# Batch attention with routing: constant part of the rows in six transfers, x statistics behind the subtraction, last groups one by one, semaphores cleared elsewhere

## The chip, the cores and the metric

The kernel runs on one core of one Trainium2 chip. The metric is the device time in microseconds (us) of one execution. The core has five engines that matter here: PE (TensorE, matrix products; its weight loads are PEld), DVE (VectorE), ACT (ScalarE), POOL (GpSimd) and SP (SyncE), which here only starts transfers. Transfers are started from the queues of SP, ACT and POOL and done by 16 DMA engines.

## The reference, cut to what matters

Two transformer layers with adaptive layer norm. The part that the change touches is the last half layer: attention over the batch axis (for each position, 16 rows attend to each other in 4 heads), layer norm, and a router that sends every one of the 8192 tokens to one of 8 experts.

```python
def _mha(x, Wqkv, bqkv, Wo, bo):            # x is (S, B, D), D = 128, hd = 32
    q, k, v = split(x @ Wqkv.T + bqkv)      # attention over B for each head
    att = softmax(einsum('bhqd,bhkd->bhqk', q, k) / sqrt(hd))
    return einsum('bhqk,bhkd->bhqd', att, v) @ Wo.T + bo
...
logits = xf @ Wg.T
idx = jnp.argmax(logits, axis=-1)
for e in range(E):                          # E = 8
    m = (idx == e)[:, None]
    h = relu(xf @ W1[e] + b1[e]);  out = out + m * (h @ W2[e] + b2[e])
```

## The kernel before, in words

`build` (line 2024) puts the stages one after the other: `prologue`, `attention` of layer 0, `token_shift_ffn`, `attention` of layer 1, `clear_semaphores`, `attend_and_route`, `run_experts`. Each stage is a block of its own: every engine has its own written program, all engines meet at the block's end, and the next block starts from there. `clear_semaphores` (line 2058) is a block with one instruction on POOL, which resets the semaphores that earlier stages have given back.

`attend_and_route` (line 1126), here called the stage, takes the 8192 tokens as 16 groups (0 to 15) of 4 tiles of 128 x 128. It is a software pipeline written out by hand: `run` (in the stage) counts steps s from -4 to 20, and each engine has a step function that serves several groups at once. In step s, ACT normalises group s+4 (`act_xn`), POOL scales and shifts it (`pool_scale`, `pool_h`) and prepares the residual of group s+3 (`pool_xb`), PE computes the scores of group s (`pe_scores`), q, k and v of group s+2 (`pe_qk`, `pe_v`), then the values and the output product of group s-1 (`pe_values`, `pe_out`). DVE starts the step with the rows of group s-2 (`vec_u`, line 1403), their statistics, then the softmax of group s: maximum, subtraction, (ACT takes the exponential, `act_exp`), sum, reciprocal, product, 32 x 32 transpose. The transposed probabilities go through four transfers on SP's queue (`sp_ax`, line 1366, tile ax), and `pe_values` waits for them. The bias-corrected k goes through four transfers of `sp_kx` (line 1295). Every engine does its instructions strictly in the order written, so one waiting instruction holds up all behind it.

The routing goes over rounds r of two groups each: `act_rstd` (step 2r+3), `vec_choose` (a chain of eight small DVE operations that ends in a running count, line 1450; step 2r+4), `pe_rank` (two products, step 2r+4), `vec_dest` (the row numbers, line 1472; step 2r+5). From step 5 on POOL sends the finished rows of group s-5 with `pool_row` (line 1492), four scatters of 128 rows for each group. A row has 387 numbers: u, three small ones, the residual, and a constant part gw. From step 12 (`s >= G - 4`) POOL does the scatters with waits on PE's progress between them (lines 1566 to 1577).

Two more jobs lie in the pipeline. The constant part gw is spread over all 24 slots of the ring S by a single transfer on ACT's queue at the end of ACT's step 0 (line 1537, 1.5 MB); steps 1 to 7 then send one block of padding rows each. And the layer norm statistics of x, needed by `act_xn`, are computed on DVE ahead of steps (`x_stats` in the vector program): a `bn_stats` for each tile by the table `x_groups`, and at four points (`PARTS`) six small operations (`vec_x_stats`) with two ACT activations in the middle (`act_stats`), for which ACT then waits.

Of the kernel before, what the change touches and what calls it, by code (L numbers as in the profile page):

```python
# [25 lines left out]
ALU = mybir.AluOpType  # L26
# [4 lines left out]
P = 128  # L31
TPB = T // P
NT = B * TPB
# [257 lines left out]
def attention(nc, A, K, layer):  # L291
# [8 lines left out]
    sh, scl = (SA0, CA0) if layer == 0 else (SA1, CA1)  # L300
    with ExitStack() as ctx:
# [421 lines left out]
        with nc.Block() as block:  # L723
# [83 lines left out]
            def _(pool):  # L807
                if layer == 1:
                    pool.tensor_tensor(K.gw[:, :], K.rows[:, 2, :], K.tab[:, 2, :], ALU.mult).then_inc(gw_ready, 1)
                    for t in range(3):  # L810
                        pool_rope(pool, 0, t)
# [314 lines left out]
def attend_and_route(nc, A, K, slot_row, expert):  # L1126
# [6 lines left out]
    G = NT // 4  # L1133
    UG, RG, VG = 7, 6, 5
    with ExitStack() as ctx:
# [11 lines left out]
        half = lambda r: slice(8 * (r % 2), 8 * (r % 2) + 8)  # L1147
# [41 lines left out]
        ones_set, gate_in, pads_out, pads_ready = sem("ones_set"), sem("gate_in"), sem("pads_out"), sem("pads_ready")  # L1189
# [4 lines left out]
        by_e = lambda t: t.unsqueeze(2).to_broadcast([P, 8, E])  # L1194
        ring = lambda g: slice(4 * (g % RG), 4 * (g % RG) + 4)
        pair = lambda r: slice(8 * (r % (RG // 2)), 8 * (r % (RG // 2)) + 8)
        held = lambda g: slice(4 * (g % UG), 4 * (g % UG) + 4)

        PARTS = [(-3, 2, 4), (-2, 4, 6), (1, 6, 10), (4, 10, 16)]
        x_groups = {-3: [2, 3], -2: [4, 5], -1: [6, 7], 0: [8], 1: [9], 2: [10, 11], 3: [12, 13], 4: [14, 15]}  # L1200

        def act_stats(act, part, n):
# [5 lines left out]
            act.wait_ge(rstd_ready, part + 1)  # L1208

        def vec_x_stats(v, part, n):  # L1210
# [8 lines left out]
            v.tensor_tensor(K.diff[:, n], mean0, mean1, ALU.add).then_inc(var_ready, 1)  # L1219
            v.wait_ge(std_ready, part + 1)  # L1220
# [4 lines left out]
        def act_xn(act, g):  # L1225
            wait(act, h1_ready, g)
            for t in range(4):
# [200 lines left out]
        def act_rstd(act, r):  # L1428
            act.wait_ge(var_done, 8 * r + 8)
            act.activation(uln[:, :], umv[:, half(r), 1], ACT.Ln, bias=K.eps[:, 0:1]).then_inc(uln_ready, 1)  # L1430
            act.wait_ge(uln_ready, r + 1)
            act.activation(S[:, pair(r), RS], uln[:, :], ACT.Exp, scale=-0.5).then_inc(rstd_done, 1)

        def vec_choose(v, link, r):

            ties = tie[:, :].unsqueeze(1).to_broadcast([P, 8, E])
            v.wait_ge(lg_ready, 2 * r + 2)
            v.wait_ge(rstd_done, r + 1)
            wait(v, pos_ps, r)
            v.wait_ge(sm_ready, min(2 * r + 5, G))  # L1440
            v.scalar_tensor_tensor(out=S[:, pair(r), MR], in0=umv[:, half(r), 0], scalar=-1.0, in1=S[:, pair(r), RS],
                                   op0=ALU.mult, op1=ALU.mult).then_inc(mr_done, 1)
            link(v.tensor_tensor(lg, raw[:, half(r), :], by_e(S[:, pair(r), RS]), ALU.mult))
            link(v.tensor_tensor(lg, lg, c8[:, :].unsqueeze(1).to_broadcast([P, 8, E]), ALU.add))
            link(v.tensor_reduce(best[:, :], lg, AX.X, ALU.max))
            link(v.tensor_tensor(lg, lg, by_e(best[:, :]), ALU.is_ge))
            link(v.tensor_tensor(lg, lg, ties, ALU.mult))
            link(v.tensor_reduce(first, lg, AX.X, ALU.max))
            link(v.tensor_tensor(hot[:, :, 1:9].rearrange("p e n -> p n e"), ties, by_e(first), ALU.is_equal))
# [3 lines left out]
        def pe_rank(pe, r):  # L1453

            pe.wait_ge(hot_ready, r + 1)
            if r == 0:
                pe.wait_ge(tab_in, 5 * 16)
                pe.wait_ge(ones_set, 1)
# [634 lines left out]
```

## Time and profile before

| What | us |
|---|---|
| median of 3 runs (1055.21 to 1058.4) | 1056.24 |
| the profiled execution | 1061.03 |
| its span, first to last instruction | 1059.2 |
| `attend_and_route`, first instruction to last scatter issue | 684.9 to 881.1 |
| `run_experts`, first transfer to the end | 889.5 to 1059.2 |

The rows of the views give the start of an instruction or of a merged group in us from the start of the span, its busy time, the engine, the source line, the operation and its tiles. In brackets stands how long the engine was idle before it and what ended that idle time. PE's granted clock stands as a share of full speed (1.0 is 2.4 GHz, 0.5 is 1.2 GHz). "issue" means that nothing in the profile shows what the engine waited for.

### The profile page before, as it was taken

To read this page: it belongs to the slowest core of one execution; us is meant where nothing else is said; L and a number is where in the kernel's file an instruction comes from. 1 tells how busy PE (TensorE), PEld (TensorE's weight loads), DVE (VectorE), ACT (ScalarE), POOL (GpSimd) and SP (SyncE) were. 2 spreads that over 40 slices of the span, in tenths; PEclk is the share of its full clock that TensorE was granted. 3 is DMA by queue.
4 is the path that set the end of the run, shared out by engine and by line. 5 is a ranking of instruction groups with operands and counts; after the bars stand their busy time and mean duration, and the time that the engine had idled before them with its cause. 6 is when DMAs were issued, how large, how long until landed. Compare 5 with 4: busy or idle time off the path is not lost. (4 is left out here: it accounts for less than half of the span.)

```text
span 1059.2 us, 25374 instructions
## 1 busy us (share of the span) xinstructions
PE 864.7 (82%) x5236; PEld 617.7 (58%) x5236; DVE 865.7 (82%) x2839; ACT 630.7 (60%) x1634; POOL 722.7 (68%) x626
## 2 busy tenths in 40 slices
PE   5699999999968858888889898377888631999993
PEld 4466666666546635555555555245565421999993
DVE  5599999999967967888889898657899760899995
ACT  2655555555349945767676766375665202999992
POOL 4488888888832228999999999373588462255554
PEclk9899999999989979999999999678899755999997
DMA  8520000000000000000000000273466554544420
GB/s 242 174 55 1 0 0 0 0 0 0 1 4 1 1 0 2 20 10 20 10 20 10 20 10 20 87 192 101 128 193 189 171 194 131 161 129 132 131 71 20
DMA packets 64855, 70.11 MB, mean 66 GB/s; under 512 B 8885, under 2 KB 52098, under 8 KB 64660
## 3 DMA queue, kind: packets, MB, share of 16 engines
q1 hardware_dynamic: 50612, 47.20, 16.1%
q0 software_dynamic: 6368, 16.89, 4.6%
q10 hardware_dynamic: 7792, 5.08, 1.9%
q8 instruction: 32, 0.52, 0.2%
q14 instruction: 51, 0.42, 0.1%
HBM read 32.32 MB, written 24.50 MB: 54 GB/s over the span
## 5 line engine op out<-in xcount | busy, mean ns | idle before, releaser
L472 PE MATMUL a_pS<-a_kv,utri 128*128 128x360 f32 (+3 forms) x768 | 264.8, 481 | 17.9 <-POOL a_kv L463 10.0
L463 POOL TENSOR_TENSOR a_kv<-a_qk,a_vv 128x1152 f32<-128x1152 f32 (+1 forms) x128 | 264.1, 2064 | 13.3 <-DVE a_qk L437 13.3
L472 PEld LDWEIGHTS a_pS<-a_kv,utri 128*128 128x128 f32 x768 | 136.1, 190 | 99.6 <-issue 25.3
L568 POOL TENSOR_TENSOR a_tt<-a_tt 128x576 f32<-128x576 f32 (+1 forms) x128 | 156.9, 1226 | 49.5 <-DVE a_tt L552 45.7
L552 DVE TENSOR_TENSOR a_tt<-a_pS,a_qk 128x360 f32<-128x360 f32 (+3 forms) x384 | 180.8, 526 | 10.8 <-PE a_pS L472 7.8
L1896 POOL DMA_INDIRECT out_dram<-x_o,x_place x71 | 69.1, 973 | 77.1 <-DVE x_o L1883 76.2
L580 DVE TENSOR_REDUCE a_nd<-a_tt 128x144 f32<-128x720 f32 (+3 forms) x128 | 104.3, 815 | 0.0
L518 ACT ACTIVATE a_tt<-a_pI 128x144 f32<-128x144 f32 (+1 forms) x96 | 40.1, 417 | 105.4 <-PE a_pI L480 105.3
L1492 POOL DMA_INDIRECT ys<-m_S,m_dest x64 | 63.6, 993 | 39.6 <-DVE m_dest L1472 15.1
L511 PEld LDWEIGHTS a_pO<-wgate,a_yT 128*128 128x128 f32 x256 | 44.8, 193 | 75.3 <-issue 45.3
L511 PE MATMUL a_pO<-wgate,a_yT 128*128 (+1 forms) x256 | 54.8, 296 | 31.0 <-POOL a_yT L542 22.7
L1834 PE MATMUL x_pZ<-w,x_hT 128*128 x568 | 76.5, 278 | 1.4 <-issue 1.3
L1785 ACT ACTIVATE x_w<-w 128x644 f32 x71 | 52.4, 741 | 34.0 <-PEq L1604 28.6
L1834 PEld LDWEIGHTS x_pZ<-w,x_hT 128*128 128x128 f32 x568 | 69.7, 193 | 2.1 <-issue 2.1
L409 ACT ACTIVATE a_vv<-a_pQ 128x128 f32<-128x128 f32 x122 | 33.8, 277 | 55.2 <-PE a_pQ L400 53.3
L371 ACT ACTIVATE a_xn<-X,nmr,rstd 128x128 f32 (+1 forms) x128 | 60.9, 485 | 2.0 <-DVE nmr L275 1.8
L287 DVE BATCH_NORM_STATS2 bn<-X 128x6 f32<-128x128 f32 (+1 forms) x256 | 57.4, 277 | 1.2 <-DMA X<-xs 1.1
L400 PE MATMUL a_pQ<-W,a_hT 128*128 128x384 f32 x122 | 51.5, 504 | 4.2 <-ACT a_hT L387 2.5
L455 POOL TENSOR_TENSOR a_qk<-a_ra,a_rb 128x256 f32<-128x256 f32 x64 | 46.8, 731 | 9.3 <-DVE a_rb L448 9.3
L400 PE MATMUL a_pQ<-wqkv,a_hT 128*128 128x384 f32 x122 | 50.3, 494 | 1.5 <-ACT a_hT L387 1.5
L480 PEld LDWEIGHTS a_pI<-a_R,a_qT 128*128 128x128 f32 x192 | 34.4, 189 | 28.3 <-ACT a_qT L524 11.2
L1816 ACT ACTIVATE x_hT<-x_pA,x_w 128x128 f32<-128x128 f32 x142 | 44.0, 362 | 9.1 <-PE x_pB L1808 9.1
(297 smaller groups left out, 2192.6 us busy)
## 6 DMA issues: line engine op xcount, KB each, us to landing
x_yl<-ys SPq DMA_DIRECT2D x71, 193.5 KB, 2.4
X<-xs SPq DMA_DIRECT2D x16, 256.0 KB, 5.2
kx<-m_kc SPq DMA_DIRECT2D x64, 64.0 KB
ax<-m_pc SPq DMA_DIRECT2D x64, 64.0 KB
m_S<-X SPq DMA_DIRECT2D x16, 256.0 KB, 2.8
xs<-X SPq DMA_DIRECT2D x15, 256.0 KB, 2.3
w<-in_L_ffn_W_dram SPq DMA_DIRECT2D x1, 2048.0 KB
m_S<-gw ACTq DMA_DIRECT2D x1, 1536.0 KB, 11.0
```

Of the source, the lines that this page charges most:

```text
L287: v.bn_stats(K.bn[:, ds(n, 1), :].rearrange("p a f -> p (a f)"), x[:, ds(n, 1), :].rearrange("p a f -> p (a f)"))\
L371: act.activation(xn[:, t, :], tile(K.X, 4 * b + t), ACT.Identity, bias=column(K.nmr, 4 * b + t), scale=column(K.rstd, 4 * b + t)).then_inc ...
L400: pe.matmul(bank_of(b, t, start)[:, 0:3 * P], hT[:, t * P:(t + 1) * P], wqkv, start=True, stop=True).then_inc(qkv_ps, 1)
L463: pool.tensor_tensor(kv[:, t % 2, :, :, :], kk.unsqueeze(2).to_broadcast([P, H, J, D]), vv[:, t, :, :].unsqueeze(3).to_broadcast([P, H, J, ...
L472: pe.matmul(pS[c][:, 0:(h1 - h0) * SC], K.utri[:, :], flat[:, h0 * SC:h1 * SC], start=True, stop=True).then_inc(u_done, 1)
L511: pe.matmul(pO[:, 0:P], yT[:, :], tile(K.wgate[:, 0 if layer == 0 else 2, :, :], b), start=True, stop=True).then_inc(proj_ps, 1)
L552: v.tensor_tensor(tt[:, t % 2, h0:h1, :, 0:D], pS[c][:, 0:(h1 - h0) * SC].rearrange("p (h j i) -> p h j i", i=D, j=J), q[:, h0:h1, :].unsq ...
L568: pool.tensor_tensor(tt[:, t % 2, :, :, D // 2:D], tt[:, t % 2, :, :, D // 2:D], tt[:, t % 2, :, :, 0:D // 2], ALU.add).then_inc(half_done, 1)
L580: v.tensor_reduce(nd[:, t % 2, :, :], tt[:, t % 2, :, :, D // 2:rows], AX.X, ALU.add).then_inc(red_done, 1)
L1492: pool.indirect_dma_start(out=A["ys"], out_offset=bass.IndirectOffsetOnAxis(ap=dest[:, g // 2 % 2, at:at + 1], axis=0), in_=S[:, 4 * (g % ...
L1834: mm = pe.matmul(pZ[j % 2][:, 0:P], hT[:, j % 2, c * P:(c + 1) * P], K.w2[:, ds(e, 1), c, :].rearrange("p a f -> p (a f)"), start=(c == 0) ...
L1896: pool.indirect_dma_start(out=token_rows, out_offset=bass.IndirectOffsetOnAxis(ap=place[:, j:j + 1], axis=0), in_=o[:, j % 4, :], in_offse ...
```

## The change

Four edits, all around `attend_and_route`:

1. The constant part gw is written in six transfers of 4 ring slots (256 KB), one at the end of ACT's steps 0 to 5, each with a semaphore of its own; the seven padding transfers move from steps 1 to 7 to steps 6 to 12.
2. The x statistics move. `bn_stats` of x and the small operations before ACT's part now stand within DVE's step, behind the subtraction (and behind `vec_var`); the last of the six (`vec_x_offset`) stands at the end of the step. The parts come at steps -4, -3, -1 and 3 in place of ahead of -3, -2, 1 and 4. ACT computes its two activations at the end of its step and no longer waits there; `act_xn` waits for the part that it needs. The tables that were set ahead of step 3 are set ahead of step 0.
3. Groups 14 and 15 are rounds of their own (round 7 and round 8), each with half as wide operations. Round 6 (groups 12 and 13) is chosen at the end of DVE's step 15 in place of step 16. POOL's wait on `w_ps` is for 15 groups at most, not 16.
4. The block of `clear_semaphores` goes. POOL clears one set at the start of `attention` of layer 1 and the rest in the stage, behind its last scatter.

```diff
-            if s == 0:
-                act.dma_start(S[:, :, GO:], K.gw[:, :].unsqueeze(1).to_broadcast([P, 4 * RG, P])).then_inc(gate_in, 16)
-            if 0 < s <= SLOTS - NT:
-                at = E * CAP + P * (s - 1)
+            if 0 <= s < RG:
+                act.dma_start(S[:, ring(s), GO:], K.gw[:, :].unsqueeze(1).to_broadcast([P, 4, P])).then_inc(gate_in[s], 16)
+            if 0 <= s - RG < SLOTS - NT:
+                at = E * CAP + P * (s - RG)
                 act.dma_start(A["ys"][at:at + P, :], A["k_pad"]).then_inc(pads_out, 16)
...
-        PARTS = [(-3, 2, 4), (-2, 4, 6), (1, 6, 10), (4, 10, 16)]
-        x_groups = {-3: [2, 3], -2: [4, 5], -1: [6, 7], 0: [8], 1: [9], 2: [10, 11], 3: [12, 13], 4: [14, 15]}
+        PARTS = {-4: (0, 2, 4), -3: (1, 4, 6), -1: (2, 6, 10), 3: (3, 10, 16)}
+        x_groups = {-4: [2, 3], -3: [4, 5], -2: [6, 7], -1: [8, 9], 1: [10, 11], 2: [12, 13], 3: [14, 15]}
...
             act.activation(K.rstd[:, n], K.std[:, n], ACT.Exp, scale=-0.5).then_inc(std_ready, 1)
-            act.wait_ge(rstd_ready, part + 1)
...
         def act_xn(act, g):
             wait(act, h1_ready, g)
+            wait(act, rstd_ready, sum(1 for _, lo, hi in PARTS.values() if g >= lo))
...
         def vec_step(v, s, link):
...
-            if even(s - 5):
+            if even(s - 5) and s < G:
                 vec_dest(v, link, (s - 5) // 2)
...
             if there(s - 2):
                 vec_var(v, s - 2)
-            if even(s - 4):
+            x_stats(v, s)
+            if s in PARTS:
+                v.wait_ge(stats, 4 * (PARTS[s][2] - 2))
+                vec_x_var(v, *part_of(s))
+            if even(s - 4) and s < G:
                 vec_choose(v, link, (s - 4) // 2)
             if there(s):
                 vec_total(v, s)
                 vec_reciprocal(v, s)
                 vec_probs(v, s)
                 vec_transpose(v, s)
+            if s in PARTS:
+                vec_x_offset(v, *part_of(s))
+            if s == G or s == G + 1:
+                vec_dest(v, link, s - 10)
+            if G - 1 <= s <= G + 1:
+                vec_choose(v, link, s - 9)
+            if s == G + 1:
+                vec_dest(v, link, s - 9)
...
-                    pool.wait_ge(w_ps, min(s, G))
+                    pool.wait_ge(w_ps, min(s, G - 1))
                     pool_row(pool, s - 5, 3)
...
                 run(pool, pool_step)
+                clear_semaphores(pool, left)
                 for i in range(RG):
                     pool.wait_ge(rows_out[i], 64 * ((G - 1 - i) // RG + 1))
...
-        clear_semaphores(nc)
```

DVE's program before, from the end of step 2 to the first operation of step 4 (bn<-X are the statistics of x, m_S<-m_rows_ps,m_U is `vec_u`), with the softmax and statistics of step 3 left out between the two pieces:

```order
L1358 STREAM_TRANSPOSE m_pc<-m_pn 128x512
L287 BN_STATS bn<-X 128x6 x8
L1679 MEMSET m_reset 128x72
L1680 MEMSET m_reset 128x8
L1681 COPY m_hot<-m_caps 128x8
L1403 TENSOR_TENSOR m_S<-m_rows_ps,m_U 128x4x128
...
L287 BN_STATS bn<-X 128x6 x8
L1212 TENSOR_TENSOR diff<-bn 128x24
L1213 TENSOR_TENSOR var<-bn 128x24
L1215 SCALAR_TENSOR_TENSOR std<-diff 128x24
L1218 TENSOR_TENSOR var<-var,std 128x24
L1219 TENSOR_TENSOR diff<-bn 128x24
L1222 SCALAR_TENSOR_TENSOR nmr<-diff,rstd 128x24
```

DVE's program of the change, from the subtraction of step 3 (m_sm) to the first operation of step 4:

```order
L1339 TENSOR_TENSOR m_sm<-m_pS,m_mx 128x512
L1437 BN_AGGR m_umv<-m_ubn 128x2 x4
L287 BN_STATS bn<-X 128x6 x8
L1220 TENSOR_TENSOR diff<-bn 128x24
L1223 SCALAR_TENSOR_TENSOR std<-diff 128x24
...
L1350 TENSOR_REDUCE m_sum<-m_ex 128x16
L1357 RECIPROCAL m_pS<-m_sum 128x16
L1362 TENSOR_TENSOR m_pn<-m_ex,m_pS 128x512
L1369 STREAM_TRANSPOSE m_pc<-m_pn 128x512
L1232 SCALAR_TENSOR_TENSOR nmr<-diff,rstd 128x24
L1414 TENSOR_TENSOR m_S<-m_rows_ps,m_U 128x4x128
```

Nothing stands between the transpose of one step and `vec_u` of the next any more but one small operation in step 3; the statistics stand between the subtraction and the sum.

ACT's program before, at the end of step 0 and the start of step 1 (w is the scaling of an expert's weights, std and rstd are `act_stats`):

```order
L1259 ACTIVATE m_hT<-m_pT 128x512
L1497 ACTIVATE w<-w,cols 128x512
L1537 DMA m_S<-gw 128x24x128
L1205 ACTIVATE std<-var,eps 128x16
L1207 ACTIVATE rstd<-std 128x16
L1228 ACTIVATE m_xn<-X,nmr,rstd 128x128 x4
```

The same place in the change:

```order
L1270 ACTIVATE m_hT<-m_pT 128x512
L1517 ACTIVATE w<-w,cols 128x512
L1565 DMA m_S<-gw 128x4x128
L1239 ACTIVATE m_xn<-X,nmr,rstd 128x128 x4
```

The transfer has a sixth of its size, and the two activations have moved to the end of step -1.

DVE's program of the change in the last steps, with the chain of `vec_choose` shortened to its last operation (m_upto) and `vec_dest` to its cast (m_dest). The first m_upto is round 6, at the end of step 15; before, it stood behind m_umv of step 16:

```order
L1369 STREAM_TRANSPOSE m_pc<-m_pn 128x512
...
L1468 SCALAR_TENSOR_TENSOR m_upto<-m_reset,m_hot 128x72
L1414 TENSOR_TENSOR m_S<-m_rows_ps,m_U 128x4x128
...
L1437 BN_AGGR m_umv<-m_ubn 128x2 x4
...
L1492 CAST m_dest<-m_posf 128x8
```

The row numbers of groups 12 and 13 (m_dest) now come in step 16, one step earlier, and two rounds of one group each follow.

## Rows read from the trace of the kernel before

**Rows 1.** Busy time by stretch: PE, PEld, DVE, ACT, POOL, then clock, DMA share, GB/s
```profile
752.00:756.00 4.00, 4.00 (x36) 2.37 (x36) 3.86 (x16) 0.00 (x0) 0.58 (x1) 0.50 0.22 53
756.00:820.00 64.00, 55.14 (x682) 38.15 (x680) 57.18 (x172) 40.99 (x82) 56.36 (x51) 0.99 0.62 188
```

**Rows 2.** Timeline at two block starts: start, busy, engine, line, operation, idle before
```profile
381.94 0.48 DVE L777 MEMSET a_vv<- 128x512 f32 x1 [0.47 <-PEq L1077]
...
684.94 0.43 DVE L1676 TENSOR_TENSOR m_gb<-rows,tab 128x128 f32<-128x128 f32 x1 [1.56 <-PEq L2062]
```

**Rows 3.** DMA issues of the page: KB each, median us to landing
```profile
m_S<-X SPq DMA_DIRECT2D x16, 256.0 KB, 2.8
...
m_S<-gw ACTq DMA_DIRECT2D x1, 1536.0 KB, 11.0
```

**Rows 4.** Timeline of steps 0 and 1: ACT's queue, SP's queue, PE
```profile
706.75 0.75 ACTq L1537 DMA_DIRECT2D m_S<-gw  x1
709.10 5.86 SPq L1366 DMA_DIRECT2D ax<-m_pc  x4
...
713.10 1.21 PE L1275 MATMUL m_rows_ps<-wv,m_hT 128*128 128x136 f32 x8
718.17 1.93 PE L1377 MATMUL m_pO<-ax,m_v 128*32 128x128 f32 x32 [3.85 <-DMA ax<-m_pc]
```

**Rows 5.** Timeline of DVE and PE, from step 2 to the start of step 4
```profile
727.82 0.69 DVE L1339 TENSOR_REDUCE m_sum<-m_ex 128x16 f32<-128x512 f32 x1 [0.92 <-ACT m_ex L1334]
729.29 1.19 PE L1394 MATMUL m_rows_ps<-wo,m_oT 128*128 128x136 f32 x8 [0.22 <-ACT m_oT L1385]
730.20 1.60 DVE L287 BATCH_NORM_STATS2 bn<-X 128x6 f32<-128x128 f32 x8
...
733.28 0.69 DVE L1403 TENSOR_TENSOR m_S<-m_rows_ps,m_U 128x512 f32<-128x512 f32 x1
...
737.83 0.69 DVE L1339 TENSOR_REDUCE m_sum<-m_ex 128x16 f32<-128x512 f32 x1 [0.41 <-ACT m_ex L1334]
740.20 1.60 DVE L287 BATCH_NORM_STATS2 bn<-X 128x6 f32<-128x128 f32 x8
743.22 0.18 DVE L1222 SCALAR_TENSOR_TENSOR nmr<-diff,rstd 128x24 f32<-128x24 f32 x1 [0.52 <-ACT rstd L1207]
743.32 0.69 DVE L1403 TENSOR_TENSOR m_S<-m_rows_ps,m_U 128x512 f32<-128x512 f32 x1
```

**Rows 6.** Timeline of DVE: the same small operation with POOL busy and idle
```profile
691.09 1.21 DVE L1215 SCALAR_TENSOR_TENSOR std<-diff 128x8 f32<-128x8 f32 x1
...
742.18 0.18 DVE L1215 SCALAR_TENSOR_TENSOR std<-diff 128x24 f32<-128x24 f32 x1
```

**Rows 7.** Timeline of POOL: first scatter, and two steps' first product
```profile
755.42 1.19 POOL L1492 DMA_INDIRECT ys<-m_S,m_dest  x1 [6.33 <-DVE m_dest L1472]
756.64 1.28 POOL L1235 TENSOR_TENSOR m_U<-m_xn,tab 128x512 f32<-128x512 f32 x1
...
765.35 1.28 POOL L1235 TENSOR_TENSOR m_U<-m_xn,tab 128x512 f32<-128x512 f32 x1
```

**Rows 8.** Timeline of DVE and POOL in the last steps, and SP's start of the experts
```profile
850.63 0.69 DVE L1403 TENSOR_TENSOR m_S<-m_rows_ps,m_U 128x512 f32<-128x512 f32 x1 [1.99 <-PE m_rows_ps L1394]
852.56 0.14 DVE L1441 SCALAR_TENSOR_TENSOR m_S<-m_umv,m_S 128x8 f32<-128x8 f32 x1
854.50 0.31 DVE L1450 TENSOR_TENSOR_SCAN m_upto<-m_reset,m_hot 128x72 f32<-128x72 f32 x1
...
858.25 0.97 POOL L1492 DMA_INDIRECT ys<-m_S,m_dest  x1 [1.99 <-DVE m_S L1403]
860.57 0.97 POOL L1492 DMA_INDIRECT ys<-m_S,m_dest  x1 [1.35 <-DVE m_dest L1472]
880.14 0.98 POOL L1492 DMA_INDIRECT ys<-m_S,m_dest  x1 [0.30 <-issue]
...
889.54 21.68 SPq L1760 DMA_DIRECT2D x_yl<-ys  x20
```

More of the change, by code:

```diff
@@ L1133, in attend_and_route @@
     G = NT // 4
+    left = sorted(set(nc.released_uncleared_semaphores) - set(K.cleared))
     UG, RG, VG = 7, 6, 5
@@ L1146, in attend_and_route @@
         rc, lg, first = pS[:, 0:16], pS[:, 64:64 + 8 * E].rearrange("p (n e) -> p n e", e=E), pS[:, 128:136]
-        half = lambda r: slice(8 * (r % 2), 8 * (r % 2) + 8)
+        unit = lambda g: g // 2 if g < G - 2 else g - G // 2 + 1
+        groups = lambda r: [2 * r, 2 * r + 1] if r < G // 2 - 1 else [r + G // 2 - 1]
+        tiles = lambda r: 4 * len(groups(r))
+        span = lambda r, n: slice(4 * (groups(r)[0] % n), 4 * (groups(r)[0] % n) + tiles(r))
         xn = sb("xn", [P, 4, P])
@@ L1188, in attend_and_route @@
                                                             sem("mr_done"), sem("sum_ps"))
[L1189 removed]
+        ones_set, pads_out, pads_ready = sem("ones_set"), sem("pads_out"), sem("pads_ready")
+        gate_in = [sem(f"gate_in{i}") for i in range(RG)]
         xb_in, rows_out = [sem(f"xb_in{i}") for i in range(RG)], [sem(f"rows_out{i}") for i in range(RG)]
@@ L1219, in vec_x_stats, with vec_x_offset @@
             v.tensor_tensor(K.diff[:, n], mean0, mean1, ALU.add).then_inc(var_ready, 1)
+        def vec_x_offset(v, part, n):
             v.wait_ge(std_ready, part + 1)
@@ L1428, in act_rstd @@
         def act_rstd(act, r):
-            act.wait_ge(var_done, 8 * r + 8)
-            act.activation(uln[:, :], umv[:, half(r), 1], ACT.Ln, bias=K.eps[:, 0:1]).then_inc(uln_ready, 1)
+            n = tiles(r)
+            act.wait_ge(var_done, 4 * groups(r)[-1] + 4)
+            wait(act, rstd_done, r)
+            act.activation(uln[:, 0:n], umv[:, half(r), 1], ACT.Ln, bias=K.eps[:, 0:1]).then_inc(uln_ready, 1)
             act.wait_ge(uln_ready, r + 1)
-            act.activation(S[:, pair(r), RS], uln[:, :], ACT.Exp, scale=-0.5).then_inc(rstd_done, 1)
+            act.activation(S[:, pair(r), RS], uln[:, 0:n], ACT.Exp, scale=-0.5).then_inc(rstd_done, 1)
         def vec_choose(v, link, r):
-            ties = tie[:, :].unsqueeze(1).to_broadcast([P, 8, E])
-            v.wait_ge(lg_ready, 2 * r + 2)
+            n = tiles(r)
+            ties = tie[:, :].unsqueeze(1).to_broadcast([P, n, E])
+            lgn, mine = lg[:, 0:n, :], hot[:, :, 1:1 + n].rearrange("p e n -> p n e")
+            v.wait_ge(lg_ready, groups(r)[-1] + 1)
             v.wait_ge(rstd_done, r + 1)
@@ L1455, in pe_rank @@
             pe.wait_ge(hot_ready, r + 1)
+            wait(pe, pos_read, r)
             if r == 0:
@@ L1645, in _ @@
                 act.preload_act_table_set("natural_log_exp_and_others")
-                run(act, act_step, before={k: lambda part=part, lo=lo, hi=hi: act_stats(act, part, slice(4 * lo, 4 * hi))
-                    for part, (k, lo, hi) in enumerate(PARTS)})
+                run(act, act_step)
                 act.wait_ge(pads_ready, 3)
@@ L1691, in _ @@
                 run(v, lambda v, s: vec_step(v, s, link),
-                    before={**{k: lambda k=k: before_step(k) for k in range(-4, 6)}, 12: lambda: after_step(12)})
+                    before={0: set_tables, 12: lambda: after_step(12)})
                 v.wait_ge(sum_ps, 1)
@@ L2055, in build, with clear_semaphores @@
         run_experts(nc, A, K, slot_row, expert, out)
-def clear_semaphores(nc):
-    released = sorted(nc.released_uncleared_semaphores)
-    with nc.Block() as block:
-        @block.gpsimd
-        def _(pool):
-            start = 0
-            for i in range(1, len(released) + 1):
-                if i == len(released) or released[i] != released[i - 1] + 1:
-                    pool.sem_clear(range(released[start], released[i - 1] + 1))
-                    start = i
+def clear_semaphores(pool, released):
+    start = 0
+    for i in range(1, len(released) + 1):
+        if i == len(released) or released[i] != released[i - 1] + 1:
+            pool.sem_clear(range(released[start], released[i - 1] + 1))
+            start = i
 def kernel(**inputs):
```

96 lines of the change are left out of this document (52 added, 44 removed).

## The prediction, made before the changed kernel ran

> **What bounds the kernel now.** I read the busy time by stretch first, then the timeline of every engine inside the stage. In steps 5 to 11 POOL is the bound: it is busy 56.36 of 64 us [rows 1], with gaps of a few tenths between its instructions, and the same product comes again after 765.35 - 756.64 = 8.71 us, one step [rows 7]. DVE is close behind (57.18 of 64 us). Before that, POOL waits: its first scatter comes after 6.33 us of idling, until DVE has the first row numbers [rows 7]. So steps -4 to 4 are set by the chain that leads to the row numbers of round 0 (ACT, PE at a reduced clock, DVE), and an earlier first scatter moves the whole POOL-bound stretch with it. At the end, POOL again issues the last 16 scatters one every 1.28 us from 860.57 to 880.14 (19.57 / 15 = 1.30, one of them longer), and the experts' first transfer starts at 889.54 [rows 8]. So the questions are how much earlier the first scatter comes, and how much earlier the last run of 16 starts.
>
> I count the shift of each point against before; negative is earlier. "so far" is the running sum.
>
> **The block that goes.** DVE idles 0.47 us into the block of layer 1's attention, but 1.56 us into the stage, with the clearing block between [rows 2]. The difference, 1.1 us, is taken: so far -1.1. Bounds: 0 and -1.6. The clear itself now costs POOL one instruction at two places. In layer 1's attention it stands ahead of gw, which is not read before the stage; in the stage it stands behind the last scatter issue, where 889.54 - 881.12 = 8.4 us pass while rows land and the blocks change [rows 8]. Taken as 0; without that cover it costs at most the 1.1 us of the whole block, twice.
>
> **Steps -3 to 0.** `act_xn` of group 2 loses its wait for the statistics, which frees ACT, but PE's products set the next steps; I estimate 0.3 us gained. The two activations of part 2 now stand at the end of ACT's step -1, in a stretch where ACT has no slack: about 0.6 us lost (two activations and the wait between; half a microsecond is also what DVE waits for such a pair, 0.52 [rows 5]). The tables set ahead of step 0 fall in DVE's wait for the first scores. So far -0.8; bounds -2.0 (no loss, 0.9 gained) and -0.2.
>
> **Step 1, the 1.5 MB transfer.** It is issued at 706.75 and lands after 11.0 us, at about 717.8 [rows 3, 4]. The four ax transfers of step 0 are issued from 709.10, take 5.86 us to be issued, and PE's `pe_values` starts at 718.17, after 3.85 us of waiting for them [rows 4]: both land together. A piece of 256 KB should take about 2.8 us, as the residual of that size does [rows 3], so it is down before or just as the first ax starts. Late next is PE itself: it ends the v products at 713.10 + 1.21 = 714.3 [rows 4], and `pe_values` follows at once. That is 3.6 us earlier in addition to the 0.8: so far -4.4. Below, nothing (0) if something else holds ax; above, another 1.5 us if PE's clock rises sooner in the denser stretch.
> The Trainium skill speaks against this step: "DMA: Bandwidth & Descriptors", section on queues, rings and completion order, says that each DMA engine takes turns packet by packet between the queues that have work. By that rule ax, on another queue, would not wait for the end of gw. The trace does not look like it (both land at 718), but if ax is slow for a reason of its own, the 3.6 us stay; that is a rival below.
>
> **Step 2.** The statistics of two groups (1.60 us for 8 tiles [rows 5]) now stand between subtraction and sum, where DVE waited 0.92 us for the exponential [rows 5]. 1.6 - 0.9 = 0.7 lost.
> **Start of step 3.** PE has the product for `vec_u` at 729.29 + 1.19 = 730.48, but `vec_u` runs at 733.28, behind the statistics at 730.20 and the tables [rows 5]. These 2.8 us go. Late next is DVE's own transpose. So far -4.4 + 0.7 - 2.8 = -6.5.
> **Start of step 4.** From 740.20 to 743.32 stand statistics and part 3, 3.1 us, ahead of `vec_u` [rows 5]: gone. In their place step 3 gets 1.6 us of statistics and about 1.0 us of small operations (3.1 without the 0.52 us wait), against 0.41 us of waiting that they cover [rows 5]: 2.2 us added. Net -0.9. The five small operations read two tiles each, and with POOL busy such an operation took 1.21 us where it takes 0.18 with POOL idle [rows 6]. Before, part 3 ran while POOL was idle; now POOL works beside it. I take half a stall, 0.5 us; bounds 0 and 5 times 1.0 us. So far -6.5 - 0.9 + 0.5 = -6.9.
> The Trainium skill gives the stall as a rule ("SBUF — State Buffer", "SBUF: two separate sides"): VectorE and GpSimd share a port pair as an exclusive lock held for a whole instruction. The 1.21 against 0.18 us agree [rows 6]. By that rule an operation can wait for a whole POOL product.
>
> **Steps 4 to 15.** Step 4 and `vec_dest` of round 0 are unchanged, so the first scatter moves from 755.42 to about 748.5. From there POOL's 8.71 us a step hold, and the shift is carried. The padding transfers, now in steps 6 to 12, are as many as before and hide behind POOL; the 256 KB pieces of steps 1 to 5 take the place that they had. Taken as 0; at most 1 us, for an ax that comes later.
>
> **The tail.** The last scatter of group 11 waited for the product of group 15: 1.99 us idle where 0.30 is the plain gap [rows 8]. With 15 in place of 16 that wait is over: 1.7 us. The next scatter, the first of group 12, waited 1.35 us for the row numbers [rows 8]: 1.05 us more. Together 2.7 us, if the row numbers of round 6 are there by 860.57 - 2.7 = 857.9 (on the old clock). They are: the choice takes 852.56 to 854.81, 2.25 us [rows 8]. Put ahead of `vec_u` at 850.63 it fills the 1.99 us of idle time [rows 8] and delays `vec_u` by some 0.3 us; rank and `vec_dest` follow in step 16, at about 854. Rounds 7 and 8 add one more chain of 2.25 us and one `vec_dest`, with the scatters of group 14 due 8 x 1.28 = 10.2 us and of group 15 15.4 us after the start of the run, both late enough to hide them (round 8 is ready near 866, due at 873). So far -6.9 - 2.7 = -9.6. Bounds for the tail: 0, and -3.5.
>
> **The experts** are unchanged and start as much earlier.
>
> Sum: -1.1 + 0.3 - 3.6 + 0.7 - 2.8 - 0.9 + 0.5 - 2.7 = -9.6 us. Against its own time the profiled execution would go from 1061.03 to 1051.4; it lay 4.8 us above the median of the runs, so I take the same 9.6 us off 1056.24: 1046.6 us.
>
> **The rivals.**
> *A, the statistics collide with POOL.* Three or four of the small operations in steps -1 and 3 each wait for a whole POOL product [rows 6]: some 3.5 us given back. For it: DVE has no slack in step 3. Against: POOL is itself idle for half of each step here. 1050.1. By the skill's lock rule this is the case to expect when POOL is busy.
> *B, ax is not held by gw.* The engines take turns between the queues, the wait at 718.17 stays, and 3.6 us are not gained. For it: two different queues, and the issue itself is slow. Against: the two land together. 1050.2.
> *C, the tail gives nothing,* since landing of the rows or the extra round sets the end: 1046.6 + 2.7 = 1049.3. Against: nothing but 0.30 us gaps between the last scatters [rows 8].
> *D, slower.* In steps 5 to 11 PE is busy 55.14 of 64 us at clock 0.99 [rows 1], 7.5 us of a step of 8.71. Just before, the clock is 0.50, and 4 of 4 us are busy [rows 1]. If with the new timing the reduced clock reaches into these steps, PE needs some 15 us in such a step and becomes the bound, 6.3 us lost for each. From two steps on (12.6 us) the gain is gone; three give 1046.6 + 18.9 = 1065.5. For it: the clock falls to that level and rises again several times in this stage. Against: PE waits less than before.
> *E, no change:* early gains are absorbed by a wait that is not visible, such as x arriving, and the tail's too: 1056. Against: DVE and POOL themselves are the things waited for.
>
> **How the numbers follow.** Forecast 0.60 (its own range 1044.0 to 1049.0), A 0.15, B 0.10, C 0.07, D 0.05, E 0.03. The range that should hold the time 8 times in 10 takes in A, B and C and the larger gains of the bounds, not D and E: 1043.0 to 1051.0. A measurement of this kernel tells a change from none from about 0.3% on, 3.2 us. Forecast, A, B and C are all faster by more: 0.92. Same 0.03, slower 0.05.
>
> **What would show it.** Right: `pe_values` of step 1 with no long wait for ax, and near 713.8 in the new trace; `vec_u` of steps 3 and 4 straight behind the transpose; the first scatter near 748.5; 8.71 us a step behind it; 16 or more scatters in a row at 1.28 us at the end, the last near 870.5; the experts near 880. Wrong: a stage start that has not moved, small operations of 1.2 us in step 3, waits for ax in step 1, a POOL that waits for m_dest in the tail, or a clock of 0.5 within steps 5 to 11.

## The result, and the profile after

| | us |
|---|---|
| median of the runs before, same chip and hour | 1057.32 (4 runs) |
| median of the runs of the change | 1046.84 (4 runs, 1041.91 to 1048.08) |
| ratio, 95% interval | 0.9878 [0.9847, 0.991] |
| profiled execution of the change, its span | 1047.97, 1046.2 |
| profiled execution before | 1061.03, 1059.2 |

A second measurement of the same two kernels gave 0.9862 [0.9835, 0.9889]. In ratio the change is worth 13 to 15 us (0.0122 x 1057 and 0.0138 x 1059), forecast 9.6. The ratio is not the quotient of the two medians, which is 0.9901 here and 0.9866 in the second measurement: by the medians the change is worth 10.5 and 14.2 us.

The same programs reach the stage at different times: its first operation on DVE (m_gb) lies at 684.94 us in before [rows 2], and between 681.35 and 685.46 in nine profiles of kernels whose programs are the same up to there. So I count every point of the stage from that operation, and use two profiles of each kernel. Negative shifts are earlier; the forecast stands here without the 1.1 us of the block, which lies ahead of it.

| behind the stage's start, us | before, two profiles | change, two profiles | shift | forecast |
|---|---|---|---|---|
| first scores' maximum | 18.56, 18.55 | 20.17, 20.15 | +1.6 | +0.3 |
| `pe_values` of step 1 | 33.23, 32.93 | 29.46, 29.47 | -3.8, -3.5 | -3.3 |
| `vec_u` of step 2 | 38.18, 36.94 | 32.58, 32.59 | -5.6, -4.3 | -3.3 |
| `vec_u` of step 3 | 48.34, 46.87 | 40.71, 40.71 | -7.6, -6.2 | -5.4 |
| `vec_u` of step 4 | 58.38, 56.93 | 48.86, 48.85 | -9.5, -8.1 | -5.8 |
| first scatter | 70.48, 69.04 | 61.63, 61.65 | -8.9, -7.4 | -5.8 |
| first scatter of group 12 | 175.63, 177.33 | 162.40, 160.81 | -13.2, -16.5 | -8.5 |
| last scatter | 195.20, 196.90 | 181.56, 180.38 | -13.6, -16.5 | -8.5 |
| experts' first transfer | 204.60, 206.41 | 190.99, 189.83 | -13.6, -16.6 | -8.5 |

The experts then take 171.0 and 169.9 us to the end of the span, 169.7 and 169.0 before: about 1 us given back.

The block: DVE idles 0.49 us into the stage, 1.56 before [rows 2], as into any block now. From the timeline of DVE in the change (start, busy, engine, line, operation, idle before), the stage's first operation and the start of step 0:

```profile
684.24 0.43 DVE L1708 TENSOR_TENSOR m_gb<-rows,tab 128x128 f32<-128x128 f32 x1 [0.49 <-PEq L724]
...
703.03 0.91 DVE L1232 SCALAR_TENSOR_TENSOR nmr<-diff,rstd 128x16 f32<-128x16 f32 x1 [4.50 <-ACT rstd L1216]
...
704.41 0.69 DVE L1334 TENSOR_REDUCE m_mx<-m_pS 128x16 f32<-128x512 f32 x1
```

This is the loss at the first scores: DVE stands 4.50 us at the last small operation of part 2, behind ACT's two activations, then needs 0.91 us for it and 0.5 us for the tables; the maximum of the scores follows at once, so the scores were there already.

Steps 0 and 1 of the change, timeline of ACT's queue, SP's queue and PE, the answer to [rows 4]; then the issues of the page, the answer to [rows 3]:

```profile
706.50 0.75 ACTq L1565 DMA_DIRECT2D m_S<-gw  x1
709.00 3.27 SPq L1377 DMA_DIRECT2D ax<-m_pc  x4
...
711.43 1.09 PE L1286 MATMUL m_rows_ps<-wv,m_hT 128*128 128x136 f32 x8
713.70 1.08 PE L1388 MATMUL m_pO<-ax,m_v 128*32 128x128 f32 x32 [1.18 <-DMA ax<-m_pc]
```

```profile
m_S<-X SPq DMA_DIRECT2D x16, 256.0 KB, 3.1
...
m_S<-gw ACTq DMA_DIRECT2D x6, 256.0 KB, 3.0
```

The four ax are issued in 3.27 us where it took 5.86, PE waits 1.18 us for them where it was 3.85, and the products themselves take 1.08 us where it was 1.93 [rows 4]: they run at TensorE's full clock.

Steps 2 to 4 on DVE in the change, the answer to [rows 5]:

```profile
716.82 0.69 DVE L1414 TENSOR_TENSOR m_S<-m_rows_ps,m_U 128x512 f32<-128x512 f32 x1 [1.51 <-PE m_rows_ps L1405]
...
724.95 0.65 DVE L1414 TENSOR_TENSOR m_S<-m_rows_ps,m_U 128x512 f32<-128x512 f32 x1
...
728.25 1.61 DVE L287 BATCH_NORM_STATS2 bn<-X 128x6 f32<-128x128 f32 x8
729.89 0.21 DVE L1220 TENSOR_TENSOR diff<-bn 128x24 f32<-128x24 f32 x1
...
730.56 0.19 DVE L1227 TENSOR_TENSOR diff<-bn 128x24 f32<-128x24 f32 x1
730.67 0.68 DVE L1350 TENSOR_REDUCE m_sum<-m_ex 128x16 f32<-128x512 f32 x1
...
733.04 0.14 DVE L1232 SCALAR_TENSOR_TENSOR nmr<-diff,rstd 128x24 f32<-128x24 f32 x1
733.10 0.68 DVE L1414 TENSOR_TENSOR m_S<-m_rows_ps,m_U 128x512 f32<-128x512 f32 x1
734.61 1.05 DVE L1430 COPY m_S<-m_ids 128x4 f32<-128x4 f32 x1
```

A step of DVE takes 8.1 us here without an idle gap. The five small operations of step 3 take 0.18 to 0.21 us each. The stall stands elsewhere: the copy at 734.61 ends at 735.66, when POOL's product ends, and the same copy in step 2 took 1.21 us (718.34). From the timeline of POOL in the change, the products around it, then the first scatter and the first products of two steps, the answer to [rows 7]:

```profile
728.01 1.28 POOL L1258 TENSOR_TENSOR X<-X,m_gb 128x512 f32<-128x512 f32 x1
734.36 1.27 POOL L1246 TENSOR_TENSOR m_U<-m_xn,tab 128x512 f32<-128x512 f32 x1 [5.08 <-ACT m_xn L1239]
...
745.87 1.19 POOL L1512 DMA_INDIRECT ys<-m_S,m_dest  x1 [7.64 <-DVE m_dest L1492]
747.08 1.29 POOL L1246 TENSOR_TENSOR m_U<-m_xn,tab 128x512 f32<-128x512 f32 x1
...
755.77 1.29 POOL L1246 TENSOR_TENSOR m_U<-m_xn,tab 128x512 f32<-128x512 f32 x1
```

The scatter comes 9.55 us earlier than in [rows 7], and the POOL-bound step keeps its length, 8.69 us. Busy time by stretch (PE, PEld, DVE, ACT, POOL, then clock, DMA share, GB/s) in the change, the answer to [rows 1]:

```profile
752.00:756.00 4.00, 4.00 (x60) 2.71 (x56) 3.83 (x19) 3.24 (x8) 3.49 (x5) 1.00 0.67 204
756.00:820.00 64.00, 53.89 (x664) 37.65 (x653) 57.59 (x171) 37.29 (x74) 53.06 (x49) 0.97 0.68 204
```

In the first stretch the clock was 0.50 and is 1.00 now. But the change is 9.55 us further in its program at that time. The same place of the program, just ahead of the first scatter, lies here:

```profile
742.50:746.50 4.00, 3.76 (x44) 2.41 (x36) 3.86 (x17) 1.42 (x3) 0.64 (x1) 1.00 0.22 51
```

The clock is 1.00 there too. In the second profile of before the same stretch (751.23 to 755.23 us) has 0.61. The tail, timeline of DVE, POOL and SP's queue in the change, the answer to [rows 8]:

```profile
839.25 0.31 DVE L1468 TENSOR_TENSOR_SCAN m_upto<-m_reset,m_hot 128x72 f32<-128x72 f32 x1
839.48 0.67 DVE L1414 TENSOR_TENSOR m_S<-m_rows_ps,m_U 128x512 f32<-128x512 f32 x1
...
844.09 0.97 POOL L1512 DMA_INDIRECT ys<-m_S,m_dest  x1 [1.06 <-PE m_pO L1388]
...
846.64 0.97 POOL L1512 DMA_INDIRECT ys<-m_S,m_dest  x1 [0.30 <-issue]
...
865.80 0.97 POOL L1512 DMA_INDIRECT ys<-m_S,m_dest  x1 [0.30 <-issue]
...
875.23 4.79 SPq L1794 DMA_DIRECT2D x_yl<-ys  x5
```

Behind 844.09 every scatter follows in 1.28 us; the waits of 1.99 and 1.35 us of [rows 8] are gone.

### The profile page after: what moved, and what is told of

Same layout as the page of the kernel before. It is cut to its first block and busy times, and to the rows that moved or that the text cites. A ratio compares the mean times of both kernels' runs of the same rounds, so it can differ in the third digit from the quotient of the medians.

```text
span 1046.2 us, 25423 instructions
## 1 busy us (share of the span) xinstructions
PE 860.2 (82%) x5240; PEld 618.0 (59%) x5240; DVE 867.7 (83%) x2853; ACT 631.7 (60%) x1636; POOL 721.6 (69%) x626
```

## The experiments

A ratio is always to the kernel before, measured beside it; the change stands at 0.9878 and 0.9862, so about 0.987. The kernels were measured in three groups: first the four with one edit undone, on one chip; then, on another chip, the change once more and three variants of it; last, on that same chip, the first edit alone, before once more, the block again and one more variant. Every ratio has an interval of 0.002 to 0.003 to either side, 2 to 3 us.

**One transfer of 1.5 MB again** (with the padding at steps 1 to 7, and POOL waiting for this one transfer).

```diff
-            if 0 <= s < RG:
-                act.dma_start(S[:, ring(s), GO:], K.gw[:, :].unsqueeze(1).to_broadcast([P, 4, P])).then_inc(gate_in[s], 16)
+            if s == 0:
+                act.dma_start(S[:, :, GO:], K.gw[:, :].unsqueeze(1).to_broadcast([P, 4 * RG, P])).then_inc(gate_in[0], 16)
```

> The changed kernel with only its first edit undone: one 1.5 MB transfer of the constant part at step 0, padding at steps 1 to 7. Theory T (ax waits for the big transfer): pe_values of step 1 is at about 717 to 718 again with more than 2 us of waiting for ax, the first scatter comes 3.5 to 5 us later than in the changed kernel (near 750), total 3 to 5 us longer. Rival B (ax is slow for its own reasons): pe_values stays near 713.7, total unchanged. Rival K (the surplus over the forecast is PE's clock, which stayed at full speed between 709 and 745): the clock falls to half near 710 again, and about 6 us are lost, of which about 2 are slower products.

Measured: 1053.71 us, 0.9922 [0.9902, 0.9943]. SP's queue and PE in steps 0 and 1, and the busy time of two stretches there:

```profile
709.94 5.73 SPq L1377 DMA_DIRECT2D ax<-m_pc  x4
712.37 1.09 PE L1286 MATMUL m_rows_ps<-wv,m_hT 128*128 128x136 f32 x8
718.93 1.93 PE L1388 MATMUL m_pO<-ax,m_v 128*32 128x128 f32 x32 [5.47 <-DMA ax<-m_pc]
```

```profile
709.00:718.00 9.00, 4.24 (x45) 2.66 (x45) 6.16 (x16) 3.98 (x9) 4.19 (x4) 1.00 0.90 232
718.00:724.00 6.00, 5.07 (x45) 4.02 (x45) 0.11 (x1) 2.74 (x6) 0.00 (x0) 0.53 0.40 101
```

PE does the v products at full clock (1.09 us), stands 5.47 us for ax, and the next products run at a clock of 0.53: 1.93 us in place of 1.08. The large transfer holds ax, and behind the wait PE runs at about half clock. The first scatter comes 67.84 us behind the stage's start, 6.2 later than in the change (3.5 to 5 expected).

The Trainium skill's rule ("DMA: Bandwidth & Descriptors", "Queues, rings and completion order") is that an engine takes turns packet by packet between its queues. Read as in the prediction, ax would then not have waited for the end of gw, which is rival B. In effect it did: the wait is 3.85, 5.26 and 5.47 us in the three profiles with one transfer ahead, 1.18 and 1.20 us with a piece of 256 KB. The measurement decides that the size of the transfer ahead sets the wait; whether the turns are taken and the large transfer still gets most of them, no run here separates.

**The statistics where they were.**

```diff
-        PARTS = {-4: (0, 2, 4), -3: (1, 4, 6), -1: (2, 6, 10), 3: (3, 10, 16)}
+        PARTS = {-3: (0, 2, 4), -2: (1, 4, 6), 1: (2, 6, 10), 4: (3, 10, 16)}
```

(with the old places of `bn_stats`, ACT's wait and the tables ahead of step 3)

> The changed kernel with only its second edit undone: x statistics and their small operations ahead of the steps, ACT waiting for them, tables ahead of step 3. Theory T: vec_u of steps 3 and 4 each stand 2.8 to 3.1 us behind what PE has ready, the first scatter comes 3 to 4 us later than in the changed kernel (near 749), total 3 to 4 us longer. The rival (DVE has other slack, the statistics cost nothing where they stood): total unchanged within 1 us. If the edit also cost something at step 0 (first maximum 0.9 us late behind the tables), vec_max of group 0 is about 0.5 to 0.9 us earlier here.

Measured: 1054.24 us, 0.994 [0.9917, 0.9964]. DVE at the end of step 3:

```profile
733.24 1.60 DVE L287 BATCH_NORM_STATS2 bn<-X 128x6 f32<-128x128 f32 x8
...
736.25 0.18 DVE L1233 SCALAR_TENSOR_TENSOR nmr<-diff,rstd 128x24 f32<-128x24 f32 x1 [0.52 <-ACT rstd L1216]
736.36 0.69 DVE L1414 TENSOR_TENSOR m_S<-m_rows_ps,m_U 128x512 f32<-128x512 f32 x1
```

The 3.1 us stand ahead of `vec_u` again. `vec_u` of steps 2, 3 and 4 lies at 33.86, 43.59 and 53.63 us behind the start, the change at 32.58, 40.71, 48.86. By step 4 the edit is worth 4.8 us, forecast about 2.2; 3.5 us are left at the first scatter (65.11), as expected, but the measured time says about 7 us (0.994 - 0.987), where 3 to 4 were expected. The first scores' maximum comes 18.72 us behind the start, 1.4 earlier than in the change: that is what the edit costs at step 0.

**Pairs of groups to the end.**

```diff
-        groups = lambda r: [2 * r, 2 * r + 1] if r < G // 2 - 1 else [r + G // 2 - 1]
+        groups = lambda r: [2 * r, 2 * r + 1]
...
-            if s == G or s == G + 1:
-                vec_dest(v, link, s - 10)
-            if G - 1 <= s <= G + 1:
-                vec_choose(v, link, s - 9)
-            if s == G + 1:
-                vec_dest(v, link, s - 9)
...
-                    pool.wait_ge(w_ps, min(s, G - 1))
+                    pool.wait_ge(w_ps, min(s, G))
```

> The changed kernel with only its third edit undone: eight rounds of two groups, the choice of groups 12 and 13 in step 16, POOL's wait for 16 output products. Theory T: first scatter unchanged (near 745.9), the last scatter 2.7 us later than in the changed kernel relative to the first, with an idle time of 1.4 us for m_dest and 2.0 us for the last product; total 2.7 us longer. Rival C (the landing of the rows or the table chain sets the end): total unchanged.

Measured: 1052.62 us, 0.9909 [0.9885, 0.9934]. POOL at the end:

```profile
851.27 0.97 POOL L1510 DMA_INDIRECT ys<-m_S,m_dest  x1 [1.99 <-DVE m_S L1414]
853.60 0.97 POOL L1510 DMA_INDIRECT ys<-m_S,m_dest  x1 [1.36 <-DVE m_dest L1490]
```

Both waits of [rows 8] are back: 1.99 and 1.36 us where the plain gap is 0.30, so 2.75 us, the forecast 2.7. The measured 4 us (0.9909 - 0.987) hold it within the intervals. The profile shows more than that: the last scatter comes 127.9 us behind the first, 119.9 and 118.7 in the change, so 8 to 9 us later where 2.7 were expected. A wait of 1.88 us for row numbers ahead of step 12 is one part, steps 12 to 15 are 2.6 to 3.5 us longer, and the cause of that was not found. That the two waits come back is shown; that they are all the edit is worth is not.

**The clearing block back**, run twice.

```diff
-                    clear_semaphores(pool, K.cleared)
...
-                clear_semaphores(pool, left)
...
+        everything = sorted(nc.released_uncleared_semaphores)
+        with nc.Block() as block:
+            @block.gpsimd
+            def _(pool):
+                clear_semaphores(pool, everything)
```

> The changed kernel with only its fourth edit undone: one block ahead of the stage that clears all semaphores. Theory T: 1.1 us of idle time more at the start of the stage, gw in layer 1's attention 0.6 us earlier without effect, end of the stage unchanged after the last scatter; total 1.1 us longer. Rival: the clear behind the last scatter or ahead of gw costs as much as the block did, total unchanged.

> The changed kernel with the clearing block back, once more. Theory: the block costs what its two idle times show, 1.1 us, and the 4 to 5 us of its first measurement came from a stretch in the middle (first scatter to row12.0: 104.9 us where the changed kernel has 99 to 101) that differs by chance: now 1.1 to 2 us slower than the changed kernel, ratio to before 0.988. Rival: a block more, or the clears of the set in one place, really costs 4 us or more: ratio 0.990 to 0.991 again, and the stretch in the middle again near 105 us.

Measured: 1052.38 us, 0.9907 [0.9882, 0.9931], then 1050.77 us, 0.9892 [0.9864, 0.992]; the second is 1.35 us above the last kernel below (tables and pieces moved, no block), measured beside it. The stage starts as in the change: the first scatter comes 61.35 and 61.60 us behind the start. The rest is lost in the middle. Ahead of step 12 POOL waits for row numbers twice in the second profile and once in the first (1.89 us), and in neither profile of the change:

```profile
781.02 0.97 POOL L1511 DMA_INDIRECT ys<-m_S,m_dest  x1 [1.87 <-DVE m_dest L1491]
...
799.97 0.97 POOL L1511 DMA_INDIRECT ys<-m_S,m_dest  x1 [1.87 <-DVE m_dest L1491]
```

Such waits stand in profiles without the block too (the two experiments on tables and pacing below). So 1.1 us is supported by the idle times and by the second measurement, and whether the block costs more stays open.

**The change once more.**

> The changed kernel again, unaltered, as the control beside the others: the ratio to before should again be about 0.988, and its profile tells how far the stretch between the first scatter (61.6 us behind the stage's start) and the scatters of group 12 (100.8 us later in its first profile) varies by itself: theory V (that stretch varies by 2 to 4 us between executions) expects 102 to 105 us here; theory T without variation expects 100.8 again.

Measured: 1045.26 us, 0.9862 [0.9835, 0.9889]. Its landmarks are in the second columns of the table above, within 0.05 us of the first up to the first scatter.

**The pieces one step later** (`0 <= s - 1 < RG`, `ring(s - 1)`, the padding after them).

> The changed kernel with each of the six transfers of gw, and the padding, one step later, so that none lies beside the ax transfers of step 0. Theory T (the transfer on ACT's queue holds ax up): the 1.18 us wait of pe_values in step 1 goes, vec_u of group 0 comes about 1 us earlier, and total up to 1 us shorter. Rival B (ax takes so long by itself): the wait stays at 1.2 to 1.4 us, total unchanged.

Measured: 1044.92 us, 0.9868 [0.9842, 0.9893], no difference. PE of step 1:

```profile
713.83 1.08 PE L1388 MATMUL m_pO<-ax,m_v 128*32 128x128 f32 x32 [1.29 <-DMA ax<-m_pc]
```

Here no piece of gw has been issued yet (the first is at 715.54 us), and PE waits as long (1.29 us). So the 1.2 us that are left are not gw's; ax has them of itself, or of other transfers.

**The tables in step -1, ahead of the last small operation of part 2.**

```diff
+            if s == -1:
+                set_tables()
...
-                run(v, lambda v, s: vec_step(v, s, link),
-                    before={0: set_tables, 12: lambda: after_step(12)})
+                run(v, lambda v, s: vec_step(v, s, link, set_tables), before={12: lambda: after_step(12)})
```

> The changed kernel with the tables set in DVE's step -1 between the statistics and the last small operation, where DVE waits 4.5 us for ACT, in place of ahead of step 0. If the first maximum is late because of them, vec_max of group 0 comes about 0.5 us earlier and so does all behind it in steps 0 and 1; total 0 to 0.5 us shorter. The rival (ACT's two activations in step -1 set it alone): vec_max unchanged.

Measured: 1043.13 us, 0.9853 [0.9827, 0.9879]. DVE at the start of step 0:

```profile
700.20 0.86 DVE L1232 SCALAR_TENSOR_TENSOR nmr<-diff,rstd 128x16 f32<-128x16 f32 x1 [2.87 <-ACT rstd L1216]
700.98 0.68 DVE L1334 TENSOR_REDUCE m_mx<-m_pS 128x16 f32<-128x512 f32 x1
```

The maximum follows the small operation at once, 19.63 us behind the start (change 20.17), and the first scatter at 61.19 (61.63): half a microsecond gained there, which the intervals don't separate from the change.

**No waits between the last scatters** (POOL's waits on `s_ps`, `o_ps` and `w_ps` from step 12 on are dropped).

> The changed kernel without POOL's three waits on PE's progress between the scatters from step 12 on. POOL idles some 13 us there. Theory P (the pacing is pure loss): the scatters run up to the next row numbers (m_dest), the last four start at about 853 in place of 862, total 6 to 8 us shorter. Rival Q (the scatters' writes slow the ax and kx transfers on which steps 12 to 15 wait, and the row numbers come later): the choice of the last groups slips by 2 to 5 us, total 0 to 4 us shorter or longer.

Measured: 1045.05 us, 0.9865 [0.9839, 0.9891], no difference, where the theory of pure loss said 6 to 8 us shorter. From step 12 on POOL waits for row numbers instead, twice, and the experts' first transfer comes 11.6 us behind the last scatter in place of 9.4 (863.52 to 875.11 us). The two waits, from the timeline of POOL:

```profile
815.69 0.97 POOL L1512 DMA_INDIRECT ys<-m_S,m_dest  x1 [1.86 <-DVE m_dest L1492]
833.73 0.97 POOL L1512 DMA_INDIRECT ys<-m_S,m_dest  x1 [8.12 <-DVE m_dest L1492]
```

The row numbers are the bound of the last steps, not the pacing: the scatters that run ahead stand 8.12 us for those of groups 10 and 11, and the first scatter of group 12 comes 161.63 us behind the start, in the change 162.40 and 160.81.

**The first edit alone in the kernel before** (six transfers, nothing else).

> The kernel before, with the first edit alone: six transfers of 256 KB with six semaphores. If the whole step-1 gain comes from the transfer (theory), pe_values of step 1 no longer waits 3.85 us for ax, TensorE's granted clock in 709 to 717 us behind a stage start at 684.5 is back near 1.00 where before has 0.77, vec_u of group 0 comes 5 to 6 us earlier, and all of it is carried: 5 to 6 us faster, ratio 0.995. Rival: the edit only works together with the moved statistics (without them another wait takes its place): 0 to 2 us faster, ratio 0.998 to 1.000. The costs of undoing each edit alone sum to more than the whole gain, so a value below 6 us would show overlap between the edits.

Measured: 1058.88 us (12 runs, 1052.81 to 1068.55), 0.9973 [0.9953, 0.9994]: 2.9 us faster, between the two theories. PE of step 1, POOL's waits for row numbers, then the busy time of two stretches:

```profile
714.69 1.08 PE L1378 MATMUL m_pO<-ax,m_v 128*32 128x128 f32 x32 [0.67 <-DMA ax<-m_pc]
...
770.70 0.98 POOL L1493 DMA_INDIRECT ys<-m_S,m_dest  x1 [1.58 <-DVE m_dest L1473]
...
792.75 0.98 POOL L1493 DMA_INDIRECT ys<-m_S,m_dest  x1 [4.33 <-DVE m_dest L1473]
...
811.74 0.97 POOL L1493 DMA_INDIRECT ys<-m_S,m_dest  x1 [1.88 <-DVE m_dest L1473]
```

```profile
755.00:775.00 20.00, 17.28 (x150) 11.84 (x154) 13.26 (x44) 10.53 (x23) 16.97 (x16) 0.74 0.58 178
...
800.00:815.00 15.00, 13.29 (x108) 8.44 (x105) 12.23 (x39) 7.00 (x15) 11.90 (x12) 0.77 0.54 168
```

The step-1 gain is there: the wait is 0.67 us, the clock is full, the first scatter comes 65.53 us behind the start (before 70.48 and 69.04). But in this execution the clock falls twice within steps 5 to 11 (0.74 and 0.77), row numbers come late, and the first scatter of group 12 is 116.7 us behind the first one, before 105.2 and 108.3. That is the mechanism of rival D, at a smaller price: 1.3 to 4.0 us above the plain gap for each such wait, not 6.3. The profiled execution is the slowest of the 12 (1068.55 us), so how often this happens, and whether it is what the median lacks, is not shown.

**The kernel before once more**, for a second profile.

> The kernel before once more, for a second profile. Theory: its clock in the stretch from 709 to 717 us (counted with a stage start at 684.9) is again clearly below 1.00 and pe_values of step 1 takes about 1.9 us and waits 3 us or more for ax; from the first scatter to row12.0 again about 105 us with a wait for m_dest of about 2 us in the middle. Rival: both were chance of one execution: then the clock is 1.00 there in this profile, or the stretch takes 100 to 101 us as in the changed kernel.

Measured: 1062.76 us, one run. PE and POOL, then the busy time of one stretch:

```profile
712.20 1.09 PE L1275 MATMUL m_rows_ps<-wv,m_hT 128*128 128x136 f32 x8
718.54 1.94 PE L1377 MATMUL m_pO<-ax,m_v 128*32 128x128 f32 x32 [5.26 <-DMA ax<-m_pc]
...
773.86 0.97 POOL L1492 DMA_INDIRECT ys<-m_S,m_dest  x1 [1.86 <-DVE m_dest L1472]
```

```profile
718.50:728.00 9.50, 9.46 (x124) 6.97 (x125) 5.05 (x20) 6.08 (x12) 3.54 (x3) 0.85 0.26 64
```

Mixed: the expected clock below 1.00 ahead of the products is not there (the v products take 1.09 us), but the wait of 5.26 us is, and the products behind it run at half clock, as with the single transfer in the change. The wait of 1.86 us at 773.86 is back, too.

**Tables in step -1 and pieces one step later together.**

> The changed kernel with the tables set in step -1, between the small operations of part 2, in place of ahead of step 0, and the six gw transfers one step later. Theory: the first takes 0.7 to 0.9 us off (the wait for ACT covers the tables), the second changes nothing: ratio 0.9855 to 0.986 to before. Rival: what is gained at the start is lost again before the first scatter, since TensorE or ACT set step 0: no difference to the changed kernel, 0.9865.

Measured: 1049.42 us, 0.9888 [0.9864, 0.9911]. The first scatter comes 61.09 us behind the start, half a microsecond before the change's, and the time shows nothing of it. No version was found that beats the change by more than the measurement tells.

## Why the prediction was right, and where it was not

The direction and the steps hold; the time (1046.6 forecast, 1046.84 measured) agrees more closely than the sum deserves, since the forecast 9.6 us stand against 13 to 15 in ratio, 10.5 and 14.2 by the medians, and 13.1 between the two profiled executions. That closeness is luck: several terms were too small, and other runs of the change lie down to 1041.91. Point by point:

- **The block, -1.1.** The idle time fell from 1.56 to 0.49 us. The stage starts at 683.7 us on average in the nine profiles without the block and at 685.3 in the five with it, but single starts differ by up to 5 us. What the whole edit is worth in time is not settled beyond that.
- **Steps -3 to 0, +0.3: mis-sized.** The first scores' maximum came 1.6 us late. Part 2's last operation waits 4.50 us for ACT, and the tables do not fall in DVE's wait, they stand behind it. It cost little at the end: the tables' move gave back 0.5 us up to the first scatter. In the second pair of profiles PE's v products came only 0.6 us late (27.18 and 26.59 us behind the start), where PE then waited for ax anyway.
- **Step 1, -3.6.** Confirmed: the single transfer in the change brings a wait of 5.47 us, the pieces alone in before take it down to 0.67. One term was missing: PE's clock after such a wait. The second pair of profiles shows it alone: -3.5 at `pe_values`, -4.3 one step later, and the products' 1.94 - 1.08 = 0.86 us are the difference.
- **Step 2 and the start of step 3, +0.7 - 2.8 = -2.1.** Measured -2.0 and -1.8 from `vec_u` of step 2 to that of step 3.
- **Start of step 4, -0.9 + 0.5 = -0.4: mis-sized.** Measured -1.9. The statistics' five operations met no stall, since POOL is idle from 729.29 to 734.36. Where POOL was busy, a copy ended with POOL's product (734.61 + 1.05 against 734.36 + 1.27), and where it was idle the operations took 0.2 us. The trace agrees here with the lock of the Trainium skill ("SBUF — State Buffer", "SBUF: two separate sides"). The forecast had the place of POOL's work wrong, not the rule. Another 0.7 us came where no edit is: the copy of the small numbers in step 3, which met POOL before (1.03 us), took 0.30. Step 4 gave 0.7 us back (from `vec_u` of step 4 to the first scatter 12.77 us, 12.10 before).
- **Steps 4 to 15, carried: mis-sized.** The 8.7 us a step hold. But before, the second pair of groups followed the first by 19.2 us in both profiles (a wait of 1.86 us for row numbers), the change by 17.6 in both, with the clock at 1.00 from 745 to 805 us. I had taken the stretch as bound by POOL throughout and not asked for its waits. Those 1.6 us are the smaller part. From the first scatter to that of group 7, where step 12 begins, the change needs 61.1 us in both profiles, before 62.8 and 63.2; from there to group 12 it needs 39.7 and 38.1, before 42.4 and 45.1. So steps 12 to 16 gained 2.7 to 7.0 us where the tail's 2.7 were forecast. Both kernels have waits for row numbers there, in other places in each profile, and what shortened them was not found. This stretch also differs from execution to execution: 99 to 102 us in the profiles of the change and of its four variants with the tables, the pieces or the pacing changed; two of them waited for row numbers before step 12 as well.
- **The tail, -2.7.** The two waits are gone, and they come back with pairs of groups. What else steps 12 to 16 gained stands in the point above.
- **The experts, 0:** 1 us given back. Over all fourteen profiles the experts take 168.2 to 171.0 us, so this need not come from the change.

Rival A (collision) and B (ax not held) fell by the rows above, C (the tail gives nothing) by the experiment with pairs, E (no change) by the time. D did not happen in the change, but did in the one profile of the first edit alone.

Undoing one edit costs about 5.5, 7.4, 4.1 and 2.3 to 4 us by ratio, together 19 to 21 us and so more than the whole gain; and the first edit alone gives 2.9. So the edits do not seem to add up, though with 2 to 3 us of interval on each this is not beyond the noise. A reading of it, not shown by an experiment of its own, is that late row numbers and a low clock turn up in the next place when one of them is removed, as in the first edit alone. The split by edit is good to 2 or 3 us only, since the four undo kernels were measured at another time and on another chip than the change's second measurement, and the ratio of the change and of its near copies lies between 0.9853 and 0.9888.

## What to carry to other kernels

A large transfer that nobody waits for can be the longest item on the path: look at what is issued behind it, on any queue, and cut it into pieces if a small transfer lands with it. Small two-operand DVE operations belong where POOL is idle. Look for the waits of the bounding engine one by one before a stretch is called carried, and count from the stage's own first operation, since its start moves by several microseconds between executions.

## What the runs showed of the hardware beyond this

- Ahead of PE's waits of 5.26 and 5.47 us for ax its products ran at full clock (1.09 us); those behind took 1.93 to 1.94 us, the level of 1.2 GHz. Ahead of the wait of 3.85 us they took 1.21 us, behind it 1.93. Behind waits of 0.67 to 1.45 us they took 1.08 us.
- The issue of the four ax on SP's queue took 5.86, 5.55 and 5.73 us with the 1.5 MB transfer ahead of it on ACT's queue, and 2.77 to 3.53 us in the eleven other profiles: SP's instruction stream is held too.
- A copy of 128 x 4 numbers on DVE took 0.15 us with POOL idle and up to 1.99 us in the POOL-bound steps of the change; there POOL is the bound, and it cost nothing that shows.
